# The last store of a Swin block kernel, split by rows over SyncE's and ScalarE's queues

## What is computed

```python
xn = _ln2d(x, norm1_g, norm1_b)
xn = jnp.roll(xn, shift=(-SHIFT, -SHIFT), axis=(2, 3))
windows = _window_partition(xn, win)             # 64 windows of 64 tokens
attn_out = _mha(windows, in_w, in_b, out_w, out_b)   # 8 heads of 8
attn_out = attn_out @ proj_w.T + proj_b
y = jnp.roll(_window_reverse(attn_out, ...), shift=(SHIFT, SHIFT), axis=(2, 3))
y = shortcut + y
z = _ln2d(y, norm2_g, norm2_b)
z = gelu(fc1(z)); z = fc2(z)                     # 64 -> 256 -> 64 channels
return y + z
```

## Time and profile before

| what | us |
|---|---|
| median of three runs | 87.67 |
| the three runs | 87.19, 87.67, 383.6 |
| the profiled execution's own time | 87.16 |
| its span, first to last instruction | 85.1 |
| granted TensorE clock over the span | 1.00 of full speed |

### The profile page before, as it was taken

The page is one execution under the profiler, slowest core; times in us unless marked ns, Lnnn a source line. Parts: engine busy times, 40 slices in busy tenths (PEclk is TensorE's granted clock), DMA queues, the critical chain, the costliest instruction groups (busy, mean ns, idle before and its releaser), DMA issues.

```text
span 85.1 us, 3859 instructions
## 1 busy us (share of the span) xinstructions
PE 78.6 (92%) x1578; PEld 45.1 (53%) x1578; DVE 65.1 (76%) x208; ACT 52.9 (62%) x89; POOL 54.1 (64%) x66
## 2 busy tenths in 40 slices
PE   5997999989999999899999979999999999999950
PEld 5984757446865665564674635555454423333420
DVE  4999998969689989989989899998743954333260
ACT  0396898979888476588297436543697755725400
POOL 7988829998982872999684696996717054700000
PEclk9999999999999999999999999999999999999999
DMA  0999600111110213100221110000000000032142
GB/s 20 210 313 428 281 31 8 46 50 53 47 53 16 72 32 115 32 23 31 82 82 54 37 46 8 0 8 8 0 0 0 0 8 0 0 123 84 39 161 85
DMA packets 3488, 5.71 MB, mean 67 GB/s; under 512 B 944, under 2 KB 1712, under 8 KB 3344
## 3 DMA queue, kind: packets, MB, share of 16 engines
q1 hardware_dynamic: 2608, 3.08, 10.9%
q10 hardware_dynamic: 864, 2.40, 7.8%
HBM read 2.66 MB, written 1.05 MB: 44 GB/s over the span
## 4 chain that ended last, share of the span: by engine, by line
PE 66%; DVE 17%; issue 8%; DMA 3%; ACT 2%; SPq 1%; DVEq 0%; ACTq 0%
PE ps_s L332 14%; PE ps_u L426 8%; PE ps_u L496 5%; PE ps_m L306 4%; PE ps_t L332 3%; PE ps_t L480 3%; PE ps_t L409 3%; DMA masked<-qk 3%; PE ps_m L295 3%; PE ps_s L480 2%; PE ps_o L440 2%; PE ps_o L496 2%; DVE sums L675 2%; DVE masked L821 2%; PE ps_o L449 2%
## 5 line engine op out<-in xcount | busy, mean ns | idle before, releaser
L656 DVE TENSOR_REDUCE row_max<-ps_s 128x16 f32<-128x1024 f32 x15 | 18.1, 1206 | 2.3 <-PE ps_s L332 2.1
L1058 POOL TENSOR_TENSOR max_x<-max_t,early 128x512 bf16<-128x512 bf16 x14 | 14.7, 1047 | 7.5 <-DVE max_t L669 7.5
L915 ACT ACTIVATE probs<-ps_t 128x1024 f32<-128x1024 f32 x13 | 13.3, 1024 | 8.8 <-PE ps_t L409 8.4
L332 PE MATMUL ps_s<-masked,qk 32*64 32x256 f32 x240 | 16.4, 386 | 1.2 <-DVE row_max L656 0.5
L332 PE MATMUL ps_t<-masked,qk 32*64 32x256 f32 x224 | 15.3, 387 | 0.0
L1067 POOL TENSOR_TENSOR rstd<-y_var,minus_half 128x4 f32<-128x4 f32 x8 | 8.3, 1033 | 7.2 <-DVE y_var L719 7.2
L332 PEld LDWEIGHTS ps_s<-masked,qk 32*64 32x64 f32 x240 | 8.1, 131 | 5.6 <-issue 2.5
L426 PE MATMUL ps_u<-probs,vz 128*32 128x64 f32 x512 | 10.5, 222 | 0.0
L426 PEld LDWEIGHTS ps_u<-probs,vz 128*32 128x32 f32 x512 | 7.9, 109 | 3.4 <-issue 3.1
L1043 POOL TENSOR_TENSOR rstd<-var,minus_half 128x4 f32<-128x4 f32 x8 | 8.4, 1054 | 1.0 <-DVE var L644 0.4
L675 DVE STREAM_TRANSPOSE sums<-ps_u 128x512 f32<-128x512 f32 x8 | 5.6, 704 | 2.8 <-PE ps_u L426 2.8
(11 more groups left out here) (115 smaller groups left out, 149.6 us busy)
## 6 DMA issues: line engine op xcount, KB each, us to landing
masked<-qk SPq DMA_DIRECT2D x38, 32.0 KB, 1.9
x_ch<-x_ch_d ACTq DMA_DIRECT2D x1, 1024.0 KB, 8.2
out_d<-result SPq DMA_DIRECT2D x3, 256.0 KB, 2.5
x_tok<-x_tok_d ACTq DMA_DIRECT2D x1, 512.0 KB, 6.2
masked<-qk SPq DMA_DIRECT2D x8, 64.0 KB, 2.5
late<-late_d ACTq DMA_DIRECT2D x1, 352.0 KB, 5.3
x_tok<-x_tok_d SPq DMA_DIRECT2D x2, 128.0 KB, 3.3
x_tok<-x_tok_d ACTq DMA_DIRECT2D x1, 256.0 KB, 4.8
```

What stands on the lines that cost most here:

```text
L332: return nc.tensor.matmul(ps[o:o + L, g, n * TOK:(n + 1) * TOK], qk[r:r + RG, b, w, t], masked[r:r + RG, b, :, w, t], start=(n == 0), stop ...
L656: nc.vector.tensor_reduce(row_max[:, w, 0:16], score_bank(k, w)[:].rearrange("q g (h j) -> q (g h) j", j=L), axis=AX.X, op=ALU.max).then_i ...
L915: nc.scalar.activation(probs[:, w, :], scores_t_bank(k, w)[:].rearrange("q g c -> q (g c)"), ACT.Exp).then_inc(probs_done, 1)
L1058: nc.gpsimd.tensor_tensor(max_x[:, k % 2, w, :].rearrange("q (n i) -> q n i", n=16), bf16_high(max_t[:, w, :]).unsqueeze(1).to_broadcast([ ...
```

## The change

The second column half of the last step is stored as two transfers by rows instead of one. SyncE stores rows 0 to 63 of it, and counts them on `stored[3]` as before. ScalarE stores rows 64 to 127: after its last `gelu` it waits for `result_done` at 5 (the value that SyncE waits for too), issues the transfer in its own queue, and waits for its landing on a new semaphore, `last_half_stored`. SyncE waits for that semaphore too, after its other landings. The first column half and all earlier stores keep their form.

```diff
+        last_half_stored = sem("last_half_stored")
...
             for s in range(STEPS):
                 for i, (a, b) in enumerate(store_parts(s)):
+                    rows = slice(0, C if b - a < STEP and i else P)
                     sp.wait_ge(result_done, s + 1 + i)
-                    sp.dma_start(out_d[:, s * STEP + a:s * STEP + b], result[:, s % 2, a:b]).then_inc(stored[s], 16)
+                    sp.dma_start(out_d[rows, s * STEP + a:s * STEP + b], result[rows, s % 2, a:b]).then_inc(stored[s], 16)
             for s in range(STEPS):
                 sp.wait_ge(stored[s], 16 * len(store_parts(s)))
+            sp.wait_ge(last_half_stored, 16)
...
             for s in range(2, STEPS):
                 for m in range(M2):
                     gelu(s, m)
+            act.wait_ge(result_done, STEPS + 1)
+            act.dma_start(out_d[C:P, ALL - STEP // 2:ALL], result[C:P, (STEPS - 1) % 2, STEP // 2:STEP]).then_inc(last_half_stored, 16)
+            act.wait_ge(last_half_stored, 16)
```

## The result

| | before | changed |
|---|---|---|
| median of 20 runs, us | 87.34 | 87.64 |
| ratio to before, 95% interval | | 1.0043 [1.0026, 1.0060] |
| profiled execution: own time / span, us | 87.16 / 85.10 | 87.69 / 85.64 |
| last finish over, us of the span | 82.52 | 82.67 |
| from there to the span's end, us | 2.58 | 2.96 |

The change costs 0.43%, about 0.38 us; the two medians differ by 0.30. That is slower, clear of noise though well within the 2% of the forecast's classes, and inside the stated range, but it is three to four times the +0.1 us that I forecast. One execution of each kernel (383.6 and 89.5 us) was far slower than its others, and the ratio leaves it out.

The account below looks back on a forecast made before the run. The chain to the last finish at 82.52 us bounds the kernel, leaving 2.58 us, mostly latency. Terms 0 + 0.04 + 0 + 0.04 = +0.08, say +0.1, on a base of 87.4 gave 87.5 us, range 86.9 to 88.4.

Parts of the forecast that it names:

- the forecast's classes: Whole kernel's time against a 2% threshold: faster 0.02, same 0.95, slower 0.03.
- SyncE's further wait: At SyncE's end, waiting for one more semaphore costs 0 to 0.08 us; taken as +0.04.
- ScalarE's lag: In the last store, ScalarE's packets start 0 to 0.30 us behind SyncE's, mostly hidden behind the other half's data: +0.04.
- What bounds the end, and that nothing ahead of 82.52 moves: After the last finish at 82.52, only 2.58 us of issue, data, completion and exit are within the change's reach.
- The transfer on SyncE gets 64 rows: SyncE's last store, halved in rows, issues at the same point, 82.55; taken as 0, with -0.2 us as low end.
- The 0.52 us stay 0.52: In the last store, both halves together move the same rows per DMA engine, so data time stays 0.52 us.
- Two completions: At the last landing, 4-byte writes go from 16 to 32; taken as 0, bounds -0.1 to +0.3 us.
- ScalarE reaches the exit late: At the exit, ScalarE's drain follows its landing but runs beside SyncE's: 0 unless ScalarE's half lands last.
- ScalarE's half is what ends last: Rival at the last store: lag not hidden and completions interfere, +0.3 to +0.6 us, about 87.9; chance 0.18.
- Half the rows land sooner: Rival at the last store: both halves land in 1.9 us instead of 2.1, -0.2 us, 87.2; chance 0.22.
- the crossing of the completions: At the last landings, two transfers' completions get in each other's way as in the middle store, up to 0.3 us.
- Rows on fewer engines: Rival at the last store: both halves use the same 8 DMA engines, data time doubles, +0.5 us, 87.9; chance 0.06.

Follow-up runs that it names:

- e1: Changed kernel with both row halves issued by SyncE, one right behind the other, and none by ScalarE; ratio 1.0091 to the kernel before.
- e5: Changed kernel without ScalarE's transfer, so only rows 0 to 63 of the last column half are stored, by SyncE; ratio 1.0005 to the kernel before.
- e13: Kernel before with step 0 stored in four transfers of 32 rows and step 1 in two of 64, all on SyncE; ratio 0.9964 to the kernel before.
- e4: Changed kernel with even rows of the last half on SyncE and odd rows on ScalarE; ratio 0.9996 to the kernel before.
- e6: Changed kernel without SyncE's transfer, so only rows 64 to 127 of the last column half are stored, by ScalarE; ratio 0.9986 to the kernel before.
- e3: Changed kernel with the last half cut by columns, 128 rows x 128 columns each on SyncE and ScalarE; ratio 1.0010 to the kernel before.
- e7: Against the changed kernel: ScalarE stores the last step's first column half, SyncE the last one whole, 128 rows each; ratio 0.9988 to the kernel before.
- e15: e2 without SyncE's wait for the landing of ScalarE's store (ScalarE waits itself); ratio 0.9956 to the kernel before.
- e2: Changed kernel with the whole last column half, all 128 rows, issued once by ScalarE alone; ratio 0.9969 to the kernel before.
- e10: e8 without SyncE's wait for ScalarE's semaphore (ScalarE waits itself); ratio 0.9978 to the kernel before.
- e8: Changed kernel with both column halves of the last step stored by ScalarE, 128 rows each; ratio 0.9976 to the kernel before.
- e11: e10 with step 2 stored by ScalarE too, SyncE waiting only for the stores of steps 0 and 1; ratio 0.9980 to the kernel before.
- e12: e11 with the last step cut in 384 and 128 columns in products, finish and stores; ratio 1.0018 to the kernel before.
- e14: Kernel before with step 0 stored in transfers of 16, 16 and 96 rows and step 1 in 48 and 80, on SyncE; ratio 0.9981 to the kernel before.

## Why the prediction was wrong, step by step

The last landing comes 0.38 us later, counted from the last finish. In the prediction's terms, with its forecast first: SyncE's half lands later by 0, measured +0.09 (2.20 against 2.11); ScalarE's half ends behind it by +0.04, measured +0.29 (2.49 against 2.20); SyncE's further wait +0.04, measured 0. So two steps failed, the cover for ScalarE's lag above all, and the start of a 64-row transfer.

- *What bounds the end, and that nothing ahead of 82.52 moves*: right. The rest grew by 0.38 us, which is the measured change, and the cut in issue, data, completion and exit is the one in which the loss can be read.
- *"The transfer on SyncE gets 64 rows": 0, with -0.2 as the low end.* This step failed. I bounded it on the side of a gain only, because the size of a transfer was the only thing that I let vary, and took "its issue starts at the same point" for "its packets do". It measured +0.34 us at the start (the same in e1 and e5 alone, and in e13 in another place), of which the data (-0.07) and the stretch to the landing (-0.18) gave most back. The trace before had a hint that an issue's length varies with the shape: the head copies of 16 rows, every fourth partition, are issued in 0.49 us at the least and 0.59 in the median, where the stores take 0.33. I had read only their landing.
- *"The 0.52 us stay 0.52"*: wrong. The engines got the same number of 1 KB packets, but a packet of 64 neighbouring rows takes about 65 ns instead of 46, and the second half starts 0.29 us late. From the first packet to the last, both halves together took 0.73 us (83.88 to 84.61). The prediction had put this down as a sign of being wrong.
- *ScalarE's lag, 0 to 0.30, of which +0.04 shows*: this is the step that cost most. The size was right, 0.29, read from the start of the kernel. That it hides was wrong: SyncE's data ended 0.28 us ahead of ScalarE's, and the whole lag shows. The cover rested on a half needing 0.26 us and on the two together needing the 0.52 of the whole; each half took 0.44 from its own start. In e4, where packets take 46 ns again, a half takes 0.32 and the two 0.60, so slow packets aren't all of it. e6 shows that 0.28 of the lag comes from meeting and 0.01 from the queue (start 1.19 alone, where SyncE's is 1.18). The Trainium skill, "DMA: Bandwidth & Descriptors", "Issuing engines are not separate DMA queues", has a second issuer saving only sequencer time; here it saved nothing and its transfer began 0.13 (e3) to 0.28 us (e6 against the changed kernel) later than alone.
- *Two completions, 0 within -0.1 to +0.3*: -0.17, the item that eased the loss, and outside the bounds. From ScalarE's last packet to its landing pass 0.56 us instead of 0.73. It isn't by there being two, since e5 and e6, with one each, have 0.55. The prediction took from the Trainium skill, "DMA: Bandwidth & Descriptors", "Anatomy of one DMA", that the completion doesn't scale with size; that section's figures are of transfers issued by GpSimd, and here it was 0.73 us for the 128 rows, 0.55 for 64 neighbouring ones and 0.42 for 64 spread ones (e4), so by these runs it does vary with the transfer.
- *SyncE's further wait, +0.04*: 0. One wait instruction of SyncE (L281) stands behind the last landing, as before. e7 shows the price that I had allowed for, 0.07, when two do.
- *ScalarE reaches the exit late, 0*: right; the exit is 0.45 us in both.
- *The rivals.* "ScalarE's half is what ends last", +0.3 to +0.6, is what happened, and its signs too: q10's packets 0.29 us behind q1's and ScalarE's landing at 2.5. I had put 0.18 on it. The condition that I had named for it, a lag of more than SyncE's data time, was not met, 0.29 against 0.44, and it wasn't needed: data that start late and take as long end late. Of what I had priced in it, the crossing of the completions and the further wait didn't come. "Half the rows land sooner" didn't happen with 64 rows of 1 KB (2.2 and 2.5 us).
- *Rows on fewer engines*: right to doubt it. Between 83.88 and 84.17 q1 alone, with its 64 rows, held the 16 engines 76.7% busy, where 8 of them could give 50% at most.
- *The time of 87.5 us* is only 0.14 under the 87.64, and part of that is luck: I had taken 87.4 for the kernel before, whose median is 87.34.

## What to carry to other kernels

At the very end of a kernel a small transfer is mostly head and completion, some 1.6 of 2.1 us here. Cutting it in two makes each part pay these again, side by side, and the later of them sets the end. What can be taken off is the issuer's and the exit's part: 0.06 to 0.08 us of the rest, by leaving out SyncE's wait (e15 against e2, e10 against e8). If a transfer is cut, look at the issue's length and at the first packet for the new shape before the bytes: here 64 rows started 0.31 to 0.37 us later than 16, 32, 48, 96 or 128. And when two engines issue at the same moment, the second one's packets start later (0.13 us in e3, 0.28 in the changed kernel), but hardly so when 0.60 us lie between the issues (0.05 in e7 and e8). So a moment when the other is quiet, or one issuer for all, is the better choice.

## What the runs showed that I had not expected

- 64 rows and no other tried number: above.
- The time outside the span, own time less span, goes with how the transfers are dealt to the queues. In the profiled executions it is 2.05 to 2.06 us in the six kernels with 53 transfers on SyncE, 1.84 to 1.88 in the four with 52 (e2, e6, e7, e15), 1.80 with 51 (e8, e10), 1.82 with 50 (e11, e12), 2.12 with 54 (e1), and 1.97 with 56 and 57 (e14, e13). All the other executions have their own time on record too, and their span to 0.1 us. The means agree up to 53 transfers (2.05 to 2.06, 1.85 to 1.87, 1.81, 1.79 to 1.83), and single executions lie within 0.07 of them. Above 53 they scatter: e1 2.11 (1.77 to 2.24), e14 1.96 (1.86 to 2.05), e13 1.86 (1.75 to 2.01), so its profiled execution is not typical, and a rising count isn't the rule. Of the 0.2 to 0.4 us by which e2, e8 and e15 beat the kernel before, 0.19, 0.24 and 0.20 lie there and not in the span. Of e13's 0.3 us some 0.2 do; the rest of it stays open.
- What the chip does in that time stays open too. The traces have one difference behind the span: e1, e13 and e14, the three with more than 53 transfers on SyncE, show a single 8 KB packet of the kind "instruction" in queue q14, 1.7 to 1.9 us after the span's end, and no other kernel does. Whether it has to do with the scatter no run here shows.
- The 32-row stores of 2 KB rows landed in 1.7 us (e13), quicker than any other transfer of 64 KB in these runs; 64 neighbouring rows of 1 KB, the same bytes, took 2.2 to 2.5, and spread ones 1.9 to 2.2 (e4).
